# Whitening 32 images on one core: the final product as four 64x64 tiles, ten image buffers, stores issued by GpSimd

## What is computed

```
x1    = x.reshape(N, C // G, G, H, W).transpose(0, 2, 1, 3, 4).reshape(N, G, -1)
xc    = x1 - x1.mean(-1)
cov   = xc @ xc.transpose(0, 2, 1) / M + EPS * eye(G)       # M = 8 * 2304
decorr = isqrt_newton_schulz(cov, 10)                        # 10 Newton-Schulz steps, 32x32
y     = weight1 @ decorr @ xc + bias1                        # written back in x's layout
```

## Time and profile before

| | us |
|---|---|
| median of 3 runs | 597.41 (587.82, 597.41, 600.44) |
| the profiled execution | 590.64 |
| its span in the profile | 588.8 |
| PE / ACT / DVE busy | 510.4 / 348.0 / 331.0 |
| PE weight loads busy | 318.8 |
| moved by DMA | 152.63 MB, mean 259 GB/s |

### The profile page before, as it was taken

The page is one execution under the profiler, slowest core; times in us unless marked ns, Lnnn a source line. Parts: engine busy times, 40 slices in busy tenths (PEclk is TensorE's granted clock), DMA queues, the critical chain, the costliest instruction groups (busy, mean ns, idle before and its releaser), DMA issues.

```text
span 588.8 us, 25310 instructions
## 1 busy us (share of the span) xinstructions
PE 510.4 (87%) x11584; PEld 318.8 (54%) x11584; DVE 331.0 (56%) x1037; ACT 348.0 (59%) x450; POOL 0.7 (0%) x6
## 2 busy tenths in 40 slices
PE   3447899899798899979988997998989989998896
PEld 3336655566465566636555654665546655555453
DVE  6747575657366476646655664675647656652210
ACT  5643675667465576746656774675666756533445
POOL 0000000000000000000000000000000000000000
PEclk9999999999899899999999998999989999999999
DMA  8993066868667867966759786788597685443338
GB/s 321 408 422 144 3 244 228 340 242 323 244 243 218 348 254 279 353 248 251 300 193 342 287 318 203 293 291 316 213 333 283 245 302 206 164 164 161 162 160 322
DMA packets 19642, 152.63 MB, mean 259 GB/s; under 512 B 2512, under 2 KB 2512, under 8 KB 3536
## 3 DMA queue, kind: packets, MB, share of 16 engines
q1 hardware_dynamic: 9744, 75.52, 35.7%
q10 hardware_dynamic: 9792, 75.50, 31.8%
HBM read 75.51 MB, written 75.50 MB: 256 GB/s over the span
## 4 chain that ended last, share of the span: by engine, by line
PE 82%; issue 9%; DVE 4%; DMA 2%; ACT 1%; SPq 1%; ACTq 0%; DVEq 0%
PE y_ps L607 48%; PE cov_ps L590 18%; PE chain_ps L567 5%; PE chain_ps L563 5%; DMA b_col<-bias 2%; PE chain_ps L573 2%; PE shift_ps L529 1%; ACT image L307 1%; PE chain_ps L552 1%; DVE transposed L407 1%; DVE outer L439 1%; PE chain_ps L575 1%; PE chain_ps L565 1%; PE chain_ps L559 1%; PE chain_ps L561 1%
## 5 line engine op out<-in xcount | busy, mean ns | idle before, releaser
L607 PE MATMUL y_ps<-image,apply_w 128*128 128x256 f32 (+2 forms) x768 | 304.4, 522 | 1.7 <-ACT image L307 1.1
L307 ACT ACTIVATE image<-y_ps,y_bias 128x768 f32<-128x768 f32 x192 | 172.6, 899 | 182.5 <-PE y_ps L607 168.6
L407 DVE STREAM_TRANSPOSE transposed<-image 128x384 f32<-128x384 f32 x384 | 213.4, 570 | 15.1 <-issue 2.1
L590 PE MATMUL cov_ps<-transposed 128*32 128x33 f32 x9216 | 134.4, 207 | 46.9 <-issue 40.8
L290 ACT ACTIVATE image<-image,shift 128x1152 f32<-128x1152 f32 x128 | 158.5, 1249 | 13.6 <-ACT image L307 10.9
L607 PEld LDWEIGHTS y_ps<-image,apply_w 128*128 128x128 f32 x768 | 133.2, 193 | 35.4 <-ACT image L307 5.2
L590 PEld LDWEIGHTS cov_ps<-transposed 128*32 128x32 f32 x9216 | 110.0, 117 | 57.5 <-issue 50.9
L461 DVE SCALAR_TENSOR_TENSOR t_mat<-chain_ps,eye 64x32 f32<-64x32 f32 x144 | 26.0, 181 | 110.2 <-PE chain_ps L563 108.6
L563 PEld LDWEIGHTS chain_ps<-yz 32*32 32x32 f32 x576 | 20.6, 105 | 109.2 <-issue 95.0
L465 DVE COPY yz<-chain_ps 64x64 f32<-64x64 f32 x144 | 29.6, 206 | 39.1 <-PE chain_ps L567 35.8
L567 PE MATMUL chain_ps<-yz,t_mat 32*32 32x64 f32 x512 | 40.2, 234 | 4.9 <-DVE t_mat L461 3.1
(11 more groups left out here) (54 smaller groups left out, 125.0 us busy)
## 6 DMA issues: line engine op xcount, KB each, us to landing
image<-x SPq DMA_DIRECT2D x63, 1152.0 KB, 7.2
y<-image ACTq DMA_DIRECT2D x62, 1152.0 KB, 5.6
y<-image ACTq DMA_DIRECT2D x6, 384.0 KB, 3.4
image<-x SPq DMA_DIRECT2D x2, 576.0 KB, 4.2
w_nat<-weight SPq DMA_DIRECT2D x4, 4.0 KB, 10.2
b_col<-bias SPq DMA_DIRECT2D x4, 0.1 KB, 10.6
```

The costliest lines, as they stand in the source:

```text
L307: nc.scalar.activation(dst, src, ACT.Identity, bias=y_bias[:, c % 2, i:i + 1]).then_inc(y_read, 1)
L407: nc.vector.transpose(dst, xs[slot_of(c, i)][:, h, of_half:of_half + PIECE // 2]).then_inc(transposed, 1)
L590: ins = nc.tensor.matmul(cov_ps[rows, i, 0:G + 1], xt[q][:, t, 0:G], xt[q][:, t, 0:G + 1], start=q == 0 and t < BLOCKS, stop=q == IMAGE_PI ...
L607: ins = nc.tensor.matmul(y_ps[:, q % 2, bank, 0:z - a], apply_w[:, c % 2, i, :, :].rearrange("p b g -> p (b g)"), xs[slot_of(c, i)][:, h, ...
```

## The change

The output piece becomes a strip of 384 pixels of both halves. PE computes it as four products of 64 rows x 64 columns, each with 384 columns streamed: the tile of input rows 64r to 64r + 63 and output partitions 64c to 64c + 63 takes half h = r xor c and writes bank h. Half 0 comes out at its own partitions; in half 1 the two groups of 64 partitions change places, and the store puts them right. `apply_w` has its 32x32 matrix twice in a row instead of four times. The eviction writes 384 columns of both halves. A store is issued once an image's last strip is evicted, by GpSimd: half 0 in one transfer of 128 rows, half 1 in two of 64 rows. The last image is stored in three groups of two strips. There are ten buffers instead of eight; SP loads images 0 to 9 at once, and then each half of image n + 10 after the store of that half of image n. The two modes of splitting an output are gone.

```diff
--- before.py
+++ after.py
@@ -37,7 +37,7 @@
 NEWTON = 10
 PAIR = 2
 PAIRS = IMAGES // PAIR
-SLOTS = 8
+SLOTS = 10
 PERIOD = SLOTS // PAIR
 Q = PAIR * G
 SHIFT_PIXELS = PIXELS // 8
...
@@ -67,6 +67,8 @@
 DVE_TOTAL = sum(DVE_OPS)
 PLACES = [1, 2] + list(range(4, STEPS + 2))
 FLAT = PAIR * IMAGE_PIECES
+HALF = P // 2
+STRIP = PIXELS // IMAGE_PIECES
 
 STEP_AT = {place: t for t, place in enumerate(PLACES)}
 assert PLACES[-1] == 2 * FLAT
...
@@ -154,13 +156,14 @@
         t_mat = sb("t_mat", [Q, G])
         folded = sb("folded", [Q, BLOCKS, G])
 
-        apply_w = sb("apply_w", [P, 2, PAIR, BLOCKS, G])
+        apply_w = sb("apply_w", [P, 2, PAIR, 2, G])
+        parity = sb("parity", [P, 2, G])
         y_bias = sb("y_bias", [P, 2, PAIR])
         credits = sb("credits", [P, 24])
         ROW, ROOT, RECIP, TWICE, HALF_RN, HALF_ROOT, RECIP2, QUOTIENT, RSQ = (col[:, i:i + 1] for i in range(9))
 
         cov_ps = pb("cov_ps", [P, 2, BANK])
-        y_ps = pb("y_ps", [P, 2, 2, BANK])
+        y_ps = pb("y_ps", [P, 2, HALVES, BANK])
         chain_ps = pb("chain_ps", [P, BANK])
         shift_ps = pb("shift_ps", [P, BANK])
 
...
@@ -247,13 +242,15 @@
                     for b in range(BLOCKS):
                         sp.dma_start(w_nat[G * b:G * (b + 1), :], weight[0]).then_inc(consts_in, 16)
                         sp.dma_start(b_col[G * b:G * (b + 1), :], bias[0]).then_inc(consts_in, 16)
-            for r in range(IMAGES // SLOTS - 1):
-                for n in range(SLOTS):
-                    for h in range(HALVES):
-
-                        sp.wait_ge(stored[n][h], 16 * r + 16)
-                        src = x_v[SLOTS * r + SLOTS + n, :, h, :]
-                        sp.dma_start(xs[n][:, h, :], src).then_inc(loaded[n][h], 16)
+
+            def load_next(n):
+
+                for h in range(HALVES):
+                    sp.wait_ge(stored[n % SLOTS][h], 16 * (1 + h) * (n // SLOTS + 1))
+                    sp.dma_start(xs[n % SLOTS][:, h, :], x_v[n + SLOTS, :, h, :]).then_inc(loaded[n % SLOTS][h], 16)
+
+            for n in range(IMAGES - SLOTS):
+                load_next(n)
 
         @block.gpsimd
         def _(pool):
...
@@ -261,6 +258,26 @@
             pool.wait_ge(setup_pool, 1)
             nc.gpsimd.affine_select(out=eye[:], in_=eye[:], compare_op=ALU.not_equal, fill=1.0, base=0,
                                     pattern=[[-1, P]], channel_multiplier=1).then_inc(eye_ready, 1)
+
+            def store(n, pieces):
+
+                pool.wait_ge(y_read, IMAGE_PIECES * n + pieces.stop + 2)
+                cols = slice(STRIP * pieces.start, STRIP * pieces.stop)
+                slot = xs[n % SLOTS]
+                pool.dma_start(out_v[n, :, 0, cols], slot[:, 0, cols]).then_inc(stored[n % SLOTS][0], 16)
+                for rows, channels in ((slice(0, HALF), slice(HALF, P)), (slice(HALF, P), slice(0, HALF))):
+                    pool.dma_start(out_v[n, channels, 1, cols], slot[rows, 1, cols]).then_inc(stored[n % SLOTS][1], 16)
+
+            for n in range(IMAGES):
+                if n == IMAGES - 1:
+                    for q in range(0, IMAGE_PIECES, 2):
+                        store(n, slice(q, q + 2))
+                else:
+                    store(n, slice(0, IMAGE_PIECES))
+            for n in range(SLOTS):
+                for h in range(HALVES):
+                    stores = (IMAGES - n + SLOTS - 1) // SLOTS + (IMAGE_PIECES // 2 - 1 if n == (IMAGES - 1) % SLOTS else 0)
+                    pool.wait_ge(stored[n][h], 16 * (1 + h) * stores)
 
         @block.scalar
         def _(act):
...
@@ -289,34 +306,15 @@
                     act.wait_ge(loaded[slot_of(c, i)][h], 16 * (r + c // PERIOD) + 16)
                 nc.scalar.activation(part, part, ACT.Identity, bias=shift[:, i:i + 1]).then_inc(centred, 1)
 
-            def output(r, c, i, q, even):
+            def output(r, c, i, q):
 
                 m = IMAGE_PIECES * image(r, c, i) + q
-                h, o = q // PIECES, q % PIECES * PIECE
                 if i == 0 and q == 0:
 
                     act.wait_ge(chain_dve, DVE_TOTAL * (PERIOD * r + c) + DVE_TOTAL)
                 act.wait_ge(y_done, m + 1)
-                slot = xs[slot_of(c, i)]
-                if even:
-                    src = y_ps[:, q % 2, :, 0:PIECE // 2]
-                    dst = slot[:, h, o:o + PIECE].rearrange("p (t s) -> p t s", t=2)
-                else:
-                    src = y_ps[:, q % 2].rearrange("p t s -> p (t s)")[:, 0:PIECE]
-                    dst = slot[:, h, o:o + PIECE]
-                nc.scalar.activation(dst, src, ACT.Identity,
-                                     bias=y_bias[:, c % 2, i:i + 1]).then_inc(y_read, 1)
-                if by_piece(r, c, i):
-
-                    act.wait_ge(y_read, m + 1 + 2)
-                    act.dma_start(out_v[image(r, c, i), :, h, o:o + PIECE], slot[:, h, o:o + PIECE]).then_inc(
-                        stored[slot_of(c, i)][h], 16)
-                elif q % PIECES == PIECES - 1:
-
-                    act.wait_ge(y_read, m + 1 + 2)
-                    n = image(r, c, i)
-                    dst = out_v[n, :, h, :] if isinstance(n, int) else out_v[bass.ds(n, 1), :, h, :].rearrange("o p s -> p (o s)")
-                    act.dma_start(dst, slot[:, h, :]).then_inc(stored[slot_of(c, i)][h], 16)
+                nc.scalar.activation(xs[slot_of(c, i)][:, :, STRIP * q:STRIP * (q + 1)], y_ps[:, q % 2, :, 0:STRIP],
+                                     ACT.Identity, bias=y_bias[:, c % 2, i:i + 1]).then_inc(y_read, 1)
 
             def root(r, c, half):
 
...
@@ -335,7 +333,7 @@
                         root(r, c - 1, f == 2)
                     done = output_at(c, f)
                     if exists(r, done[0]):
-                        output(r, *done, evenly(r, c))
+                        output(r, *done)
                     ahead = later(c, i, 2)
                     if filling(r, c):
                         for n, what in FILL_SCALAR.get((c, f), []):
...
@@ -473,7 +460,8 @@
                     if exists(r, c - 2):
                         dve.wait_ge(y_read, IMAGE_PIECES * image(r, c - 1, 0) + 2)
                     spread = chain_ps[:, C_SPREAD:C_SPREAD + PAIR * G].rearrange("p (i g) -> p i g", i=PAIR)
-                    link(diagonal(apply_w[:, c % 2], spread, PAIR, P, BLOCKS))
+                    link(nc.vector.tensor_tensor(apply_w[:, c % 2], spread.unsqueeze(2).to_broadcast([P, PAIR, 2, G]),
+                                                 parity[:].unsqueeze(1).to_broadcast([P, PAIR, 2, G]), ALU.mult))
 
                     link(nc.vector.tensor_scalar(y_bias[:, c % 2, :], chain_ps[:, C_OFFSET:C_OFFSET + PAIR], -1.0,
                                                  b_col[:, 0:1], ALU.mult, ALU.add))
...
@@ -505,6 +493,7 @@
             for k in range(2 * IMAGE_PIECES):
                 transpose(0, 0, 0, k)
 
+            then(nc.vector.tensor_tensor(parity[:], blocks[:, 0:2, :], blocks[:, 2:4, :], ALU.add))
             then(nc.vector.tensor_scalar(mean_col[:], eye_col[:], 1.0 / SAMPLES, None, ALU.mult))
             then(nc.vector.tensor_scalar(eps_eye[:], eye_col[0:Q, :], EPS, None, ALU.mult))
             for b in range(BLOCKS):
...
@@ -591,23 +580,20 @@
                                            start=q == 0 and t < BLOCKS, stop=q == IMAGE_PIECES - 1 and t >= TILES - BLOCKS)
                 ins.then_inc(cov_done, 1)
 
-            def output(r, c, i, q, part, even):
-
-                if part == 0:
-                    if i == 0 and q == 0:
-
-                        pe.wait_ge(chain_dve, DVE_TOTAL * (PERIOD * r + c) + DVE_TOTAL)
-
-                    pe.wait_ge(y_read, IMAGE_PIECES * image(r, c, i) + q + 1)
-                h, o = q // PIECES, q % PIECES * PIECE
-                bank = 1 - part
-                a, z = BANK * bank, min(BANK * (bank + 1), PIECE)
-                if even:
-                    a, z = PIECE // 2 * bank, PIECE // 2 * (bank + 1)
-                ins = nc.tensor.matmul(y_ps[:, q % 2, bank, 0:z - a], apply_w[:, c % 2, i, :, :].rearrange("p b g -> p (b g)"),
-                                       xs[slot_of(c, i)][:, h, o + a:o + z], start=True, stop=True)
-                if part == 1:
-                    ins.then_inc(y_done, 1)
+            def output(r, c, i, q):
+
+                if i == 0 and q == 0:
+
+                    pe.wait_ge(chain_dve, DVE_TOTAL * (PERIOD * r + c) + DVE_TOTAL)
+
+                pe.wait_ge(y_read, IMAGE_PIECES * image(r, c, i) + q + 1)
+                for row in range(2):
+                    for col in range(2):
+                        rows, out_rows = slice(HALF * row, HALF * (row + 1)), slice(HALF * col, HALF * (col + 1))
+                        h = row ^ col
+                        ins = nc.tensor.matmul(y_ps[out_rows, q % 2, h, 0:STRIP], apply_w[rows, c % 2, i].rearrange("p k g -> p (k g)"),
```

(17 more changed lines are left out.)

## The result

The changed kernel took **662.3 us** (median of 4 runs, 651.6 to 672.4) against 594.2 for the kernel before (4 runs beside it): ratio **1.127, 95% interval 1.084 to 1.170**. The forecast was 566, range 475 to 612. It was wrong in sign and outside its range.

The account below looks back on a forecast made before the run. PE looked like the bound, its code arriving in blocks of 128 matmuls through the images' DMA engines. Terms summing to -29 us on a 588.8 us span gave 562, or 568 shifted to the median; forecast 566, range 475 to 612.

Parts of the forecast that it names:

- Rival C: Output tiles on PE: no overlap across rows, output stays at 1.49 us, 600 to 625 us in all; chance 0.05.
- rival A: Code fetch: the code keeps up, the DMA is the bound, 455 to 495 us in all; chance 0.17.
- Stores: Stores through GpSimd: second half lands in 5.6 to 11.2 us, covered by ten buffers; last image 1 us later.
- Code: PE's code fetch: 3.02 blocks an image instead of 2.83, 5.6 us a block, 16.9 us an image.
- images 1 to 22, -5: Middle images: 16.9 us each instead of 17.14, 5 us saved over 22 images.
- The end: Last store, the last image going by thirds through GpSimd: 0 to 2 us later, taken as +1.
- Images 24 to 31: Images after the loads: 10 us saved in images 24 to 27, 14 in images 28 to 31.
- The clock: PE's granted clock: more waits in a shorter step bring more of the low level, +4 us.
- rival D: PE's clock: low for long stretches, a block 6.0 us, nothing net, 580 to 600 us; chance 0.17.
- Rival B: Code fetch: store and two loads form one burst, blocks take 6.4 to 6.9 us, 605 to 640 us; chance 0.11.

Follow-up runs that it names:

- half_columns: The kernel before, each output matmul streaming only 192 columns on the whole array (half of the output left out): 575.5 us, ratio 0.977.
- the longer code alone: The kernel before, each output matmul cut in two by columns, whole array and 128-row stores kept: 599.1 us, ratio 1.026.
- whole-row kernel: The changed kernel, half 1 of each image stored in one 128-row transfer, its two channel groups left exchanged: 607.3 us, ratio 1.039 to the kernel before.
- the filler: The changed kernel with one more whole-array matmul of 384 columns ahead of each output: 692.6 us, ratio 1.181 to the kernel before.
- The fastest kernel: The changed kernel with the covariance of a piece in 12 matmuls of 64 x 65 instead of 24: 507.3 us, ratio 0.870 to the kernel before.

## Why the prediction was wrong

**Right:** the four tiles overlap, 0.81 us against 0.85, and a step at full clock is 1.78 us against 1.83. With the tiles the code was late next, in waits that lie whole blocks of 128 matmuls apart; their sum rose well over 40.8 us. Rival C fell: the two tiles of a diagonal write one bank and did not hold each other up. Ten buffers were worth nothing in the middle. The Trainium skill (Runtime: NRT & Kernel Launch, Instruction fetch mechanics) calls the cost of crossing a block mostly hidden; the 112 us of waits after the change speak against it again, and rival A, which rested on the code keeping up, fell.

**The step that failed** is in "Stores", and through it in "Code". The prediction had the 64-row pieces land "between the 5.6 us that the same bytes take now and 11.2", and said "Ten buffers cover both". They landed after 8.6 us, inside the bounds. The buffers did cover the delay; they could not cover the DMA time. The pieces moved at half the rate (221 GB/s against 429) and kept the engines busy 249 us instead of 187, and what waits behind the DMA was not a buffer but PE's code. The prediction had itself shown that the code comes through the same engines, and then priced the stores only by their landing. It took 5.6 us a block; measured were 6.42, and 5.72 with the pieces taken out. For the kernel with whole-row stores 5.6 was good to 2%, but in part by luck: there too only 33 of 70 blocks ended in a wait, and others were as long as they were because PE ran at the low clock (from 131 to 148 us, 332 matmuls in 17 us at 0.50, 6.55 us a block). The mis-sized term is "images 1 to 22, -5", where the pieces add 44.6 us over images 1 to 23.

**Not right even without the pieces:** the gain in the middle. At 5.72 us a block and 3.02 blocks an image is as long as before; half_columns' 13 us, less 15 for the longer code alone, say the same. More than half_columns' 13 us was won there only with shorter code (0.865, 0.870).

**The end** was taken at +1 us and measured +20.6. Moving whole-row stores to GpSimd brings 7 of it (10.5 against 3.3 after the last eviction), in the whole-row kernel 12 (15.6). In the changed kernel two parts make up most of it: the last store was issued at 634.1 us and landed at 647.5, 13.4 us later where the last pieces before took 3.4 in the median, with the DMA at 0.93 of its time from 626 to 646 for 278 GB/s; and then GpSimd's last instruction ran for 8.40 us. "0 to 2 us" bounded neither.

**Images 24 to 31** were to save 24 us and saved 0.4. With the loads gone, the code should have come every 4.4 us; images 24 to 27 took 16.4 each. The four waits behind 64-row pieces and a short one were 13.0 us of it. Without the pieces the waits were 7.1 us, yet these images took 17.2 each, at a clock of 0.67 instead of 0.84: what the waits gave back went to the low clock. In images 28 and 29 PE had no code wait, but ran at the low clock throughout (0.50 from 582 to 623 us): a step was 596.74 - 594.22 = 2.52 us where the forecast had 1.68 and the kernel before, at a clock of 1.00, 2.32.

**The clock** (+4) was mis-sized as well. It was 0.71 in the middle; it fell with the waits, as at 308.81, where PE goes on at 0.50. The prediction had it that "a slow step inside a block that waits for its code costs little". But at that level PE's own work takes 6.45 us a block, more than the 5.6 that the code was given, so such a block is long without any wait. This is rival D's mechanism (6.0 us a block), and it was at work in the changed kernel beside the waits. It does not explain the 47.6 us: with whole-row stores the clock was hardly higher (0.75) and 44.6 of them were gone. D's price of 580 to 600 fell 60 us short. How much the low clock costs by itself no run separates; the filler, which raised it, also added work.

**Rival B** named the right place, the code fetch, and the right point, over 18.7 us an image; measured 19.4. But its mechanism, one burst of a whole image out and two loads in, was not it either: the whole-row kernel has the same burst and 17.3 us an image. Its range of 605 to 640 holds that kernel, and misses the changed one.

**What stays open:** why 64 rows move at half the rate. The runs show that they cost more DMA time from three queues, with and without the exchange of channels. Also open are what the low clock costs apart from the waits, and why the last stores took so long to land.

## What to carry to other kernels

A transfer has two prices, its landing and the time that it keeps the DMA engines; buffers hide the first only, and a kernel whose code streams through the same engines pays the second in waits of "issue" on its busiest engine. Before taking work off such an engine, divide its instructions by the block and the block's period: where that product is already the stage's time, shorten the code first (here the tiles alone cost 13%, and with a shorter covariance they gave 13%). And a layout that lets PE go faster may have to leave through a worse store: cost the store by its queue's share of DMA time in a run, not by bytes. Last, waits can bring the low clock with them, and at that clock the engine's own work (here 6.45 us a block) may be the next limit.

## What was not expected of the hardware

- The same 75.50 MB kept the DMA engines 187 to 191 us in 128-row transfers and 237 to 249 us with half of the bytes in 64-row ones (221 GB/s against 429 within one image's store). ACT's issue of a 64-row store took 1.05 us in the middle, 2.53 at most, of a 128-row one 0.34.
- GpSimd's last instruction grew with the count of its transfers: 5.62 us after 68 (three kernels), 8.40 after 102 (five kernels), some 82 ns each; but 1.30 us after the 68 split ones.
- A destination in two runs of 64 rows: 67648 packets instead of 9408, a landing of 40.1 us, and on ACT 17.8 us an issue for two in a row.
- With the outputs on four tiles and no covariance PE ran at the low clock for 41 us though busy for 35.8 of them; on whole arrays, busy for 20.8 of 24 us, the kernel before kept 1.00. The fastest kernel, too, had 0.50 in that phase (an output of 1.48 us).
